# The first tap of three short convolutions, multiplied on ScalarE instead of VectorE

## The reference, cut to what matters

```python
def _short_conv(x, w):
    K = w.shape[1]
    xp = jnp.pad(x, ((0, 0), (K - 1, 0), (0, 0)))
    y = jax.lax.conv_general_dilated(xp, jnp.transpose(w)[:, None, :], (1,), 'VALID', ..., feature_group_count=w.shape[0])
    return jax.nn.silu(y)
...
q = _short_conv(hidden_states @ Wq, conv_q).reshape(B, T, H, DK)
k = _short_conv(hidden_states @ Wk, conv_k).reshape(B, T, H, DK)
v = _short_conv(hidden_states @ Wv, conv_v).reshape(B, T, H, DV)
q = _l2norm(q) * SCALE
k = _l2norm(k)
```

## Time and profile before

| | |
|---|---|
| three runs | 6653.74, 6659.9 and 6662.19 us, median 6659.9 |
| the profiled execution | 6661.47 us, span 6659.7 us |
| mean granted clock of TensorE | 0.982 of full speed |
| busy in the span | TensorE 6146.7 us (92%), VectorE 4830.9 (73%), ScalarE 2724.6 (41%), GpSimd 1811.1 (27%) |
| the convolutions on VectorE | first taps L890: 384 instructions, 239.0 us, mean 622 ns; other taps L896: 1152, 993.4 us, mean 862 ns |
| GpSimd | L1185: 896 instructions, 979.0 us; L1193: 256, 286.0 us; L1197: 256, 324.7 us |
| a table load of ScalarE (L1086, L1139) | 1283 ns |
| attention part | about 280 to 5840 us, 43 us a step |

### The profile page before, as it was taken

How to read it: one execution, slowest core, us unless ns; L and a number is a source line. 1 busy time by engine, 2 the same in 40 slices (tenths; PEclk the granted TensorE clock), 3 DMA queues, 4 the chain that set the end, 5 groups by cost and what they waited for, 6 DMA issues and landing times. The chain is left out here.

```text
span 6659.7 us, 108024 instructions
## 1 busy us (share of the span) xinstructions
PE 6146.7 (92%) x33720; PEld 4309.7 (65%) x33720; DVE 4830.9 (73%) x7947; ACT 2724.6 (41%) x4746; POOL 1811.1 (27%) x1636
## 2 busy tenths in 40 slices
PE   5699999999999999999999999999999999899999
PEld 2467766766667667766777667766777777644444
DVE  7688878888788878887888788878888888611110
ACT  2344444444444444444444444444444444401101
POOL 2233333333333333333333333333333333200000
PEclk8899999999999999999999999999999999999999
DMA  2101010100010100101010101010100000032221
GB/s 71 43 25 30 21 33 26 32 25 27 26 32 26 27 25 25 32 25 30 22 33 25 33 25 29 22 33 26 32 26 27 25 26 26 16 114 81 85 78 43
DMA packets 183592, 234.20 MB, mean 35 GB/s; under 512 B 25048, under 2 KB 128088, under 8 KB 179168
## 3 DMA queue, kind: packets, MB, share of 16 engines
q1 hardware_dynamic: 111072, 188.22, 9.7%
q10 hardware_dynamic: 72192, 41.95, 2.2%
HBM read 183.75 MB, written 46.38 MB: 35 GB/s over the span
## 5 line engine op out<-in xcount | busy, mean ns | idle before, releaser
L659 PE MATMUL bank<-xT,weights 128*128 (+1 forms) x4096 | 2183.2, 631 | 87.3 <-DMA bg_col<-in_L_attn_bg 34.6
L1185 POOL TENSOR_TENSOR KR<-KR,decay_u 128x256 f32<-128x256 f32 x896 | 979.0, 1093 | 2358.1 <-PE bank L685 2358.1
L911 DVE TENSOR_TENSOR KQ<-KQ,decay_u 128x512 f32<-128x512 f32 x896 | 759.8, 848 | 602.2 <-PE bank L685 602.0
L685 PEld LDWEIGHTS bank<-KQ,KR 128*128 128x128 f32 x7168 | 919.2, 192 | 249.7 <-issue 216.3
L896 DVE SCALAR_TENSOR_TENSOR conv<-pre,taps,conv 128x512 f32<-128x512 f32 x1152 | 993.4, 862 | 27.3
L685 PE MATMUL bank<-KQ,KR 128*128 128x128 f32 x7168 | 954.7, 276 | 1.7 <-DVE KQ L911 1.7
L659 PEld LDWEIGHTS bank<-xT,weights 128*128 128x128 f32 x4096 | 660.6, 194 | 299.4 <-issue 216.8
L931 DVE COPY_PREDICATED all_pairs<-level_mask,bank 128x512 f32<-128x512 int32 x896 | 793.4, 885 | 0.0
L707 PEld LDWEIGHTS bank<-T_inv,pairs 128*128 128x128 f32 x3072 | 457.3, 193 | 470.3 <-issue 248.3
L707 PE MATMUL bank<-T_inv,pairs 128*128 128x64 f32 x3072 | 656.0, 339 | 62.0 <-DVE T_inv L947 59.6
L1103 ACT ACTIVATE T_inv<-bank 128x256 fp32r<-128x256 f32 x640 | 248.0, 388 | 792.6 <-PE bank L722 792.6
(11 more groups left out here) (162 smaller groups left out, 9129.5 us busy)
## 6 DMA issues: line engine op xcount, KB each, us to landing
decay_u<-decay_scratch SPq DMA_DIRECT2D x128, 510.0 KB
beta_u<-beta_scratch SPq DMA_DIRECT2D x128, 256.0 KB
y_scratch<-y_out ACTq DMA_DIRECT2D x128, 256.0 KB, 6.9
y_in<-y_scratch SPq DMA_DIRECT2D x32, 1024.0 KB, 4.8
xt<-in_L_attn_hidden_states SPq DMA_DIRECT2D x8, 1024.0 KB, 5.5
x_in<-in_L_attn_hidden_states SPq DMA_DIRECT2D x32, 256.0 KB, 5.0
out<-o_out ACTq DMA_DIRECT2D x32, 256.0 KB, 2.0
w<-in_L_ffn_W SPq DMA_DIRECT2D x8, 704.0 KB, 4.9
```

The source lines that it names most:

```text
L659: last = nc.tensor.matmul(bank[w % 2][:], weights[par][:, w, k, :], xT[:, k, bass.ds(j * UC, UC)], start=k == 0, stop=k == KC - 1)
L685: last = nc.tensor.matmul(to[:, :, i], KR[:, cols(i)], halves(KQ[:, :, cols(i)], l, 1), start=True, stop=True)
L911: nc.vector.tensor_tensor(second_halves, second_halves, pair[:, :, 0:1].unsqueeze(1).to_broadcast([P, 2, blocks, 1 << l]), ALU.mult).then_ ...
L1185: nc.gpsimd.tensor_tensor(first_halves, first_halves, second.to_broadcast([P, UC >> (l + 1), 1 << l]), ALU.mult).then_inc(keys_scaled.sem, 1)
```

## The change

ScalarE gets a function `first_tap(w)`, which multiplies `pre` by the first tap with the per-partition scale of an activation, and calls it for q after `take_x(1)` (ahead of `silu_v`), for k after `take_x(3)`, and for v between the copy of delta and `silu_squares(1)`. On VectorE `convolve` loses its `tensor_scalar`; its first instruction is now tap 1, which waits for ScalarE's signal. The counts of the steps' semaphores go from 4 to 3 per convolution wherever they are waited for.

```diff
-    qk_conv_steps, v_conv_steps = signal("qk_conv_steps", 2 * TAPS), signal("v_conv_steps", TAPS)
+    qk_conv_steps, v_conv_steps = signal("qk_conv_steps", 2 * (TAPS - 1)), signal("v_conv_steps", TAPS - 1)
+    qk_first_tap, v_first_tap = signal("qk_first_tap", 2), signal("v_first_tap", 1)
...
             def convolve(w, which=range(TAPS)):
...
-                if 0 in which:
-                    if w < 2:
-                        wait(dve, qk_pre_ready, u, w + 1)
-                    else:
-                        wait(dve, v_pre_ready, u, 1)
-                    if before is not None:
-                        if w < 2:
-                            wait(dve, squares_rest_ready, before, w + 1)
-                        else:
-                            wait(dve, v_silu_ready, before, 1)
-                    nc.vector.tensor_scalar(conv[:, w], pre[:, w, :, 0:P], taps[par][:, w, 0:1], None,
-                                            ALU.mult).then_inc(steps.sem, 1)
+                steps, n = (qk_conv_steps, w * (TAPS - 1)) if w < 2 else (v_conv_steps, 0)
                 for t in which:
                     if t == 0:
                         continue
-                    wait(dve, steps, u, n + t)
+                    if t == 1:
+                        wait(dve, qk_first_tap if w < 2 else v_first_tap, u, w + 1 if w < 2 else 1)
+                    else:
+                        wait(dve, steps, u, n + t - 1)
...
+            def first_tap(w):
+                u, before, par = (a, m, s.par_a) if w < 2 else (m, b, s.par_m)
+                if u is None:
+                    return
+                ready, n, tapped = (qk_pre_ready, w + 1, qk_first_tap) if w < 2 else (v_pre_ready, 1, v_first_tap)
+                wait(act, ready, u, n)
+                if w == 1:
+                    wait(act, qk_halo_ready, u, 1)
+                if before is not None:
+                    if w < 2:
+                        wait(act, squares_rest_ready, before, w + 1)
+                    else:
+                        wait(act, v_silu_ready, before, 1)
+                nc.scalar.activation(conv[:, w], pre[:, w, :, 0:P], ACT.Copy,
+                                     scale=taps[par][:, w, 0:1]).then_inc(tapped.sem, 1)
...
             take_projection(0)
             take_t(1)
             take_x(1)
+            first_tap(0)
             silu_v()
             take_t(2)
             take_x(2)
             take_projection(1)
             take_t(3)
             take_x(3)
+            first_tap(1)
             take_t(4)
...
                 nc.scalar.activation(delta[:], bank[5][:], ACT.Copy).then_inc(delta_ready.sem, 1)
+            first_tap(2)
             silu_squares(1)
```

More of the change, by code:

```diff
@@ L617, in load_next @@
             wait(sp, gate_ready, h * J - 1, 1)
-            wait(sp, v_conv_steps, h * J - 1, TAPS)
+            wait(sp, v_conv_steps, h * J - 1, TAPS - 1)
             load_head(h + 1, 1 - par)
@@ L874, in convolve @@
             def convolve(w, which=range(TAPS)):
-                u, before, par = (a, m, s.par_a) if w < 2 else (m, b, s.par_m)
+                u, par = (a, s.par_a) if w < 2 else (m, s.par_m)
                 if u is None:
                     return
-                steps, n = (qk_conv_steps, w * TAPS) if w < 2 else (v_conv_steps, 0)
-                if 0 in which:
-                    if w < 2:
-                        wait(dve, qk_pre_ready, u, w + 1)
-                    else:
-                        wait(dve, v_pre_ready, u, 1)
-                    if before is not None:
-                        if w < 2:
-                            wait(dve, squares_rest_ready, before, w + 1)
-                        else:
-                            wait(dve, v_silu_ready, before, 1)
-                    nc.vector.tensor_scalar(conv[:, w], pre[:, w, :, 0:P], taps[par][:, w, 0:1], None,
-                                            ALU.mult).then_inc(steps.sem, 1)
+                steps, n = (qk_conv_steps, w * (TAPS - 1)) if w < 2 else (v_conv_steps, 0)
                 for t in which:
@@ L991, in unit_inputs @@
                 nc.vector.tensor_tensor(KQ[:, 1], q_hat[:], decay, ALU.mult).then_inc(unit_ready.sem, 1)
-            halo(a, s.a_first, m, qk_conv_steps, 2 * TAPS, slice(0, 2), qk_halo_ready)
-            halo(m, s.m_first, b, v_conv_steps, TAPS, slice(2, 3), v_halo_ready)
+            halo(a, s.a_first, m, qk_conv_steps, 2 * (TAPS - 1), slice(0, 2), qk_halo_ready)
+            halo(m, s.m_first, b, v_conv_steps, TAPS - 1, slice(2, 3), v_halo_ready)
             add_identity_to_z(1)
@@ L1064, in silu_squares @@
                     return
-                wait(act, qk_conv_steps, a, (w + 1) * TAPS)
+                wait(act, qk_conv_steps, a, (w + 1) * (TAPS - 1))
                 if w == 0 and m is not None:
@@ L1076, in silu_v @@
                     return
-                wait(act, v_conv_steps, b, TAPS)
+                wait(act, v_conv_steps, b, TAPS - 1)
                 nc.scalar.activation(v_u[:], conv[:, 2].rearrange("p b t -> p (b t)"),
```

## The result

The changed kernel takes 6504.6 us (median of 4 runs, 6500.3 to 6513.8) against 6660.7 before: 0.9772 of the time, 95% interval 0.9758 to 0.9787. That is 156 us less; the forecast was 6519, 142 less, in a range of 6503 to 6570. The profiled execution took 6503.2 us with a span of 6501.5, which is 158.2 under the span before.

A forecast was written before the change was run, and what follows sets the result against it. The bound was VectorE's scale(6) waiting behind GpSimd's squares_rest, idling TensorE about 1.01 us a step. 127 steps × (1.05 + 0.07) = 142 us off the profiled 6661.5 gave 6519 us; range 6503 to 6570.

The forecast's parts named there:

- The price of a tap: One first tap on ScalarE, a scaled copy from SBUF, takes 0.72 us, bounds 0.60 and 0.75.
- v's tap and what queues behind it: ScalarE's v tap ends at 3048.33; VectorE's second tap waits for it, and take_residual(0) starts 0.02 us late, harmlessly.
- The GpSimd pair moves: GpSimd's two instructions start 0.63 us later or more; squares_rest falls 0.43 us behind scale(6), instead of 0.04 ahead.
- What is late next: After scale(6), TensorE's refine product comes 1.07 us earlier, taken as 1.05; sums(1) keeps 0.29 us to spare.
- the maximum of `scale`: Sign in the profile after: VectorE's scale instruction falls from a maximum of 1.80 us to about 1.15 at most.
- 1.05 + 0.07 a step: Gain in each of 127 steps: 1.05 us from the earlier refine product, 0.07 from k's tap; 142 us in all.
- the step on k's tap: Without k's multiplication on VectorE, add_identity_to_z(6) ends earlier and TensorE's next product follows sooner: 0.07 us a step.
- Rival A: No change: TensorE hides it, scale(6) waits as long as before, only the 0.07 us is won; 6651 us, 5%.
- q's tap at nothing: q's multiplication on VectorE (0.48 us) is followed by a wait for TensorE's next level, so removing it gains 0.
- Rival B: Slower: GpSimd keeps the port between its two instructions, so scale(6) ends 0.47 us later than now; 6711 us, 5%.

The follow-up runs named there:

- tap_late: The changed kernel with one more scaled copy on ScalarE ahead of v's first tap, so that the tap ends 0.61 us later: 6580.7 us, 0.9882.
- short_copy_early: The kernel before, all taps on VectorE, with one 128-column copy on ScalarE ahead of silu_v: 6642.3 us, 0.9978.
- short_copy_silu: The kernel before, all taps on VectorE, with one 128-column copy on ScalarE ahead of the second SiLU: 6517.7 us, 0.9791.
- tap_k_only: The kernel before with only k's first tap moved to ScalarE, q's and v's left on VectorE: 6521.5 us, 0.9795.

## Why the prediction was right, and where not

- **The price of a tap**: forecast 0.72 from two differences of rows, measured 0.713 (median).
- **v's tap and what queues behind it**: right in each start to 0.03 us. L956 left where it was; the cover was just used up, as `tap_late` shows, where 0.61 us more cost 76 us.
- **The GpSimd pair moves**: right. I had L911 waiting for the end of L1193 for a moment. In fact it started 0.14 us before that end and took 0.69 all the same.
- **What is late next**: nothing, as forecast; the sums of squares cost hardly more than before: TensorE waits four times for `squares_rest`, 12.1 us in all instead of 11.4. One sign was off: I wrote that the maximum of `scale` falls to about 1.15 us. One instruction of the 896 still takes 1.77.
- **The mis-sized terms of the sum**: 1.05 + 0.07 a step, measured 1.15. I had worked out 1.07 and taken 1.05; TensorE shows 1.09 and 0.07. Over 127 steps the missing 0.03 are about 4 us. 8.9 us came at the turns of the loop and 4.0 ahead of the first step; neither was in the sum. Together they are the 16 us between 142 and the 158 of the two spans. That these two went the same way was luck; at the turns TensorE's clock was low for 43 us instead of 57.
- **What failed, though the total hid it**: the step on k's tap, "This is worth 0.07 us a step". Its direct effect is that, 0.07 to 0.08. But I did not ask what else 0.07 us would do to a pair of starts that lie 0.04 us apart, though both numbers stood in my text. Either k's tap or v's is enough for the 1.09 us, and the gain doesn't add up from its parts: 143 and 138 us alone, 156 together with q's. Rival A's condition, a tap of over 1.4 us, was not tested.
- **q's tap at nothing**: right in the steps (median 43.11 us, 43.10 before); the 14 us in the whole time stand mostly at the turns, and their cause is open.
- **Rival B**, the port not let go between two GpSimd instructions, fell with `tap_late`. **Rival A** fell with the result. VectorE's load did not bring the gain: with all taps left on VectorE, the two copies ahead of the SiLU gave 0.979 of the time just as well. The multiplication is indeed slower on ScalarE (0.713 against 0.48 us). The rule of the Trainium skill (Perfetto Trace Analysis, "Optimizing Scalar/DVE Operations") says that VectorE is faster where it has a faster mode, and that a move may make sense where it is saturated. The two times agree with the first half. The result did not hang on either half.

## What to carry to other kernels

When a wait has the same length in every step, compare the starts of the two instructions that exclude each other: at a distance of hundredths of a microsecond the order is an accident, and any edit near it, a useless copy too, can win or lose the whole wait. Then price an edit by what it does to the order, not by the work it moves, and test the parts alone, since they need not add up. An instruction that doesn't take part in the exclusion, such as one with an input in PSUM, belongs into the wait of one that does.

## What the runs showed of the hardware

- `scale(6)`, a VectorE instruction with two inputs in SBUF, takes 1.78 us when it starts 0.02 to 0.04 us behind GpSimd's `squares_rest` (the kernel before and `short_copy_early`). When it starts less than 0.01 us ahead of it, it takes 0.69, and GpSimd's takes 1.83 instead of 1.27 (`short_copy_silu`).
- When it started 0.14 us before the end of a GpSimd instruction, it took 0.69 us, so it lost nothing (the kernel after). That fits the other cases: where VectorE's instruction is the one that waits, it ends 0.54 to 0.55 us after GpSimd's end, and 0.14 + 0.55 is 0.69. Where GpSimd's `squares_rest` waits, it ends 1.13 to 1.14 us after VectorE's end (medians) (the kernel after, `tap_k_only`, `short_copy_silu`).
- It gets in between two GpSimd instructions that follow each other by 0.28 us (`tap_late`, 0.98 us).
- At the turns of the outer loop TensorE is idle for some us, and its granted clock falls to 1.2 GHz. In the 72 turns of the twelve profiled executions, those with the low clock for about 10 us cost 9.2 to 10.7 us over the kernel's median step; those with 5.3 to 6.8 us cost 5.1 to 8.5, and those with 3.4 us cost 4.5 to 6.0. Which causes which these runs don't separate.
